# State scan of an audio encoder block: the decayed states' part as one VectorE product with u, and D x summed by TensorE

## Chip, core and metric

The kernel runs on one core of one Trainium2 chip, in float32. The metric is the device time of one execution in microseconds (us). "TensorE", "VectorE", "ScalarE", "GpSimd" and "SyncE" are the core's engines; the profile calls them PE, DVE, ACT, POOL and SP.

## The reference

Three selective-scan layers with a halving of the sequence behind each of the first two, then an attention block and a mixture of experts with 16 experts, each on a normalised input with a residual. The change touches only the scan layers. The input is 32 sequences of 750 steps with 64 channels.

```python
def _ssm_layer(x, A_log, Dp, W_dbc, W_dt, b_dt):
    A = -jnp.exp(A_log)
    dbc = jnp.einsum('ble,ce->blc', x, W_dbc)
    delta, Bm, Cm = jnp.split(dbc, [DT_RANK, DT_RANK + N_STATE], axis=-1)
    delta = jax.nn.softplus(jnp.einsum('blr,er->ble', delta, W_dt) + b_dt)
    dA = jnp.exp(delta[..., None] * A)
    dBx = (delta * x)[..., None] * Bm[:, :, None, :]
    ...
    _, hs = jax.lax.associative_scan(combine, (dA, dBx), axis=1)
    y = jnp.einsum('blen,bln->ble', hs, Cm)
    return y + Dp * x
for i in range(NUM_LAYERS):
    x = _ssm_layer(x, A_log[i], D[i], W_dbc[i], W_dt[i], b_dt[i])
    if i < NUM_LAYERS - 1:
        b, l, d = x.shape
        x = x[:, :l // 2 * 2].reshape(b, l // 2, 2, d).mean(axis=2)
```

## The kernel before

**Tiling.** The 128 partitions hold 64 channels of two sequence groups. A unit is a tile of 128 x 750 (748 in the last layer) steps: 16 units in layer 0, 8 in layer 1, 4 in layer 2, 28 in all. They are taken in eight phases: six of four units (layers 0 and 1) and two of two units (layer 2). Each phase finds out which of the 64 states decay so fast that nothing is left of them a step later. Those are the "decayed" states: their part of y is local, `x * (mixed-down x) * delta`, and needs no scan. The slow ones, two per phase here, are scanned one by one ("slots" 0 and 1, `STATIC = 2`). A branch for more slots (`more_slots`) is in the code and not taken.

**What one unit computes.** With u = delta x (GpSimd, `inputs`):

- decayed part: TensorE multiplies x by a 128 x 128 matrix (`mixed`), VectorE multiplies that by x (`product`), TensorE sums over channels (`summed`), all through the PSUM tile `pairs[3]`. VectorE then multiplies it by delta in place (`by_delta`, L1328), and `output` (L1335) makes y0 = (that + D) x in one instruction. For layers 0 and 1, D and the C weights carry a factor 0.5, since the halving is a mean of two.
- scanned part, for each slot j: TensorE's `weighted_b` into `pairs[1 + j]`, VectorE's `load` (times u, L1343), `recur` (the scan, L1350) and `read` (times C, L1362, into `hC`).
- halving, layers 0 and 1: TensorE's `sums` (L557) adds even and odd columns of both `hC` tiles in one PSUM bank by four products with the identity, two ahead of `weighted_b` of slot 0 of the next unit and two behind it; ScalarE copies the bank out (`sums_out`, L1009); GpSimd adds y0's even and odd columns (L1699) and adds them to that copy (`add`, L1702). In layer 2 there is no halving, and `sums` does nothing.

**Order.** Each engine has a fixed program order, written out in its `period(n)`; semaphores tie the engines together. In a middle period n, VectorE runs load(n,0), product(n+1), recur(n,0), load(n,1), read(n,0), by_delta(n+1), recur(n,1), output(n+1), read(n,1). TensorE runs weighted_b(n,1), row products for later units (L521, L527), summed(n+1), sums(n-1) part 0, weighted_b(n+1,0), sums(n-1) part 1, mixed(n+2); `mixed` waits for `output` of the unit before, since both use `pairs[3]`. At the end of a phase TensorE does sums(n) part 0, weighted_b(n+1,1), sums(n) part 1 at once, so that the last period of a phase has both parts of two units and the first period of the next has none; that first period has the products for the next phase's extremes instead (L506, L564, which wait for VectorE's reduction L1284). GpSimd runs the three steps of delta (L1674, L1677, L1679), then u (L1684), then the halving of the unit before; in a phase's first period the halving stands between delta and u. `wide` (L484, L485) is a product over 750 columns, as 512 and 238.

SyncE brings the C and delta rows in, spread over the partitions (`spread<-rowsd`).

Of the kernel before, what the change touches and what calls it, by code (L numbers as in the profile page):

```python
# [5 lines left out]
ALU = mybir.AluOpType  # L6
# [48 lines left out]
UB = [sum(u for _, _, u in PHASES[:p]) for p in range(NP + 1)]  # L55
# [11 lines left out]


LAST = UB[NP - 1]
Z_OF = UNITS  # L70
ROWS = {-2: [(None, 0), (None, 1)]}
for _n in range(-1, UNITS - 1):
    ROWS[_n] = [(_n + 1, _n + 3 if _n + 3 < LAST else None)]
    if _n == LAST - 3:
        ROWS[_n].append((_n + 2, None))
# [6 lines left out]
def program(nc, a, out):  # L82
    SCALE = float(D) ** 0.25
    with ExitStack() as ctx:
        def sb(name, shape, dt=F32):
            return ctx.enter_context(nc.sbuf_tensor(name, shape, dt))
# [4 lines left out]
        pairs = [ctx.enter_context(nc.psum_tensor(f"pair{i}", [128, 1024], F32)) for i in range(4)]  # L91
        bank = [pairs[i // 2][:, 512 * (i % 2):512 * (i % 2) + 512] for i in range(8)]
# [5 lines left out]
        with nc.sbuf_tensor("spread", [128, 4500], F32) as spread, nc.sbuf_tensor("work", [128, 8400], F32) as work:  # L98
# [7 lines left out]
        delta, u = (big[:, at:at + 750 * RING] for at in (13500, 18750))  # L106

        packed = sb("packed", [128, PACKED])
        ident, blocks, tri, slotno, temp, w0, bdt, dskip, wdt, A = (
            packed[:, at:at + n] for at, n in zip(PACK_AT, PACK))  # L110
# [13 lines left out]
        bproj = sb("bproj", [128, 1])  # L124
        centering = sb("centering", [128, 128])
        averaging = sb("averaging", [128, 128])
        eps = sb("eps", [128, 1])
        zero = sb("zero", [128, 4])
        floor = sb("floor", [128, 16])
# [27 lines left out]
        y0T = [work[:, at:at + 750] for at in (3750, 4500, 5250)]  # L157
# [53 lines left out]
        rw_p, mx_p, s_p, b_p, pl_p = sem("rw_p"), sem("mx_p"), sem("s_p"), sem("b_p"), sem("pl_p")  # L211
        abs_a, relu_a, exp_a, log_a, one_a = sem("abs_a"), sem("relu_a"), sem("exp_a"), sem("log_a"), sem("one_a")
        dk_a, sel_a, rw_a, sm_a = sem("dk_a"), sem("sel_a"), sem("rw_a"), sem("sm_a")
        p_v, t_v, y_v = sem("p_v"), sem("t_v"), sem("y_v")
        bu_v, sc_v, hc_v = sem("bu_v"), sem("sc_v"), sem("hc_v")
        sum_g, cor_g, dl_g, u_g = sem("sum_g"), sem("cor_g"), sem("dl_g"), sem("u_g")
# [76 lines left out]
        def unit(n):  # L293

            p = PH[n]
            l, c, _ = PHASES[p]
            return p, l, WIDTH[l], xcols(l, c + (n - UB[p]) * WIDTH[l], WIDTH[l])

        def of(t, n):
            at = 750 * (n % RING)  # L300
            return t[:, at:at + WIDTH[PHASES[PH[n]][0]]]
# [37 lines left out]
        def after(eng, sem, value):  # L339
            if value > 0:  # L340
                eng.wait_ge(sem, value)

        def halves(t, l):

            if l == 0:
                s = t[:, 0:750].rearrange("p (t k) -> p t k", k=2)
                return s[:, :, 0], s[:, :, 1]
            s = t[:, 0:750].rearrange("p (b t) -> p b t", b=2)[:, :, 0:374].rearrange("p b (t k) -> p b t k", k=2)
            return s[:, :, :, 0], s[:, :, :, 1]

        def parts(t, l):

            return t[:, 0:375] if l == 0 else t[:, 0:374].rearrange("p (b t) -> p b t", b=2)
# [126 lines left out]
        def _(pe):  # L480
# [66 lines left out]

            def sums(n, part):

                _, l, _, _ = unit(n)  # L550
                if l == 2:
                    return
                if part == 0:
                    after(pe, sm_a, TAKEN[n] - 1)
                pe.wait_ge(hc_v, STATIC * n + part + 1)
                for k, t in enumerate(halves(hC[n % 2][part], l)):
                    mm = pe.matmul(parts(bank[1], l), ident, t, start=(part == 0 and k == 0),  # L557
                                   stop=(part == 1 and k == 1))
                if part == 1:
                    mm.then_inc(pl_p, 1)  # L560

# [342 lines left out]
            for l in range(LAYERS):  # L904
                pe.matmul(bank[2][0:64, 128 * l:128 * l + 128].rearrange("p (k c) -> p k c", k=2), wtok[:, l, 1:65],
                          ident[0:64, 0:64].unsqueeze(1).to_broadcast([64, 2, 64]), start=True, stop=True)
                mm = pe.matmul(bank[3][0:64, 128 * l:128 * l + 128].rearrange("p (k c) -> p k c", k=2),
                               wtok[:, l, 65:129], ident[0:64, 0:64].unsqueeze(1).to_broadcast([64, 2, 64]),
                               start=True, stop=True)
            mm.then_inc(setup_p, 1)  # L910
            pe.wait_ge(setup_v, 2)
            for l in range(LAYERS):
                mm = pe.matmul(bank[4][:, l:l + 1], wdtr[0:1, l, :], ident[0:1, 0:1], start=True, stop=True)
# [316 lines left out]
        def _(v):  # L1230
            v.sem_inc(more_v, 1)

            def setup():
                v.memset(w0pm[:, :, :], 0.0)
                v.memset(wZ[:, :, :], 0.0).then_inc(blank_v, 1)
                v.wait_ge(blank_v, 1)
                v.wait_ge(params_in, PARAMS)
                v.tensor_scalar(A, A, 88.0, None, ALU.min)
                v.tensor_scalar(AT[:, :, :], AT[:, :, :], 88.0, None, ALU.min)
                for k in range(2):  # L1240
                    blk = slice(64 * k, 64 * k + 64)
                    v.tensor_copy(w0pm[blk, :, k], w0[blk, :])
                    v.tensor_scalar(w0pm[blk, :, 2 + k], w0[blk, :], -1.0, None, ALU.mult)
                for l in range(LAYERS):
                    for k in range(2):
                        blk = slice(64 * k, 64 * k + 64)
                        ins = v.tensor_scalar(wZ[blk, l, blk], wdt[blk, l, :], w0[blk, l:l + 1], None, ALU.mult)
                ins.then_inc(setup_v, 1)
                for k in range(2):
                    ins = v.tensor_copy(wdtr[:, :, 64 * k:64 * k + 64], wdt[0:1, :, :])  # L1250
                ins.then_inc(setup_v, 1)
                v.tensor_scalar(dskip[:, 0:2], dskip[:, 0:2], 0.5, None, ALU.mult)
                v.tensor_scalar(fscale[:, 0:8], temp, SCALE, None, ALU.mult)
                v.wait_ge(setup_p, 1)
                v.tensor_copy(wBT[:, :, :].rearrange("p l c -> p (l c)"), bank[2][0:64, 0:384])
                v.tensor_scalar(wCT[:, 0:2, :].rearrange("p l c -> p (l c)"), bank[3][0:64, 0:256], 0.5, None, ALU.mult)
                v.tensor_copy(wCT[:, 2, :], bank[3][0:64, 256:384])
                v.wait_ge(setup_p, 2)
                v.tensor_copy(wdtc[:, :], bank[4][:, 0:LAYERS])
                v.wait_ge(setup_a, 2)  # L1260
                v.tensor_scalar(A, A, -1.0, None, ALU.mult)
                v.tensor_scalar(AT[:, :, :], AT[:, :, :], -1.0, None, ALU.mult).then_inc(setup_v, 1)
                v.wait_ge(zeroed, 2)
# [58 lines left out]
                v.tensor_tensor(PT[:, 0:w], pairs[3][:, 0:w], x, ALU.mult).then_inc(p_v, 1)  # L1322

            def by_delta(n):
                _, _, w, _ = unit(n)
                v.wait_ge(s_p, n + 1)
                v.wait_ge(dl_g, n + 1)
                v.tensor_tensor(pairs[3][:, 0:w], pairs[3][:, 0:w], of(delta, n), ALU.mult).then_inc(t_v, 1)  # L1328

            def output(n):  # L1330

                _, l, w, x = unit(n)
                v.wait_ge(t_v, n + 1)
                after(v, xa_g, n - 2)
                v.scalar_tensor_tensor(y0T[n % 3][:, 0:w], pairs[3][:, 0:w], dskip[:, l:l + 1], x, ALU.add, ALU.mult)\  # L1335
                    .then_inc(y_v, 1)

# [557 lines left out]
```

## Time and profile before

| | us |
|---|---|
| median of 3 runs (lowest, highest) | 811.09 (809.99, 812.42) |
| the profiled execution | 812.87 |
| its span in the trace | 810.7 |
| start to the end of unit 0's last instruction on VectorE | 48.67 |
| units 1 to 3 | 32.73 |
| units 4 to 23, five phases of four | 219.35 |
| units 24 to 27 (layer 2) | 55.46 |
| attention and experts | 454.39 |
| TensorE, VectorE, ScalarE, GpSimd busy over the span | 89%, 68%, 52%, 54% |

A stretch's borders are ends of the last `read` (L1362) of a unit on VectorE. In the trace a float32 product shows as two matmul records, so "x4" at L557 is two products. Instructions on one engine overlap at their ends: what one of them takes of the engine is the distance from its start to the next one's start, which is shorter than its duration.

### The profile page before, as it was taken

The page shows a single profiled execution, that of the slowest core. Times are in us where ns is not written, and L with a number is a line of the kernel's source. Part 1 is how long each engine was busy: PE and PEld are TensorE (multiplying, and loading weights), DVE is VectorE, ACT ScalarE, POOL GpSimd, SP SyncE. Part 2 cuts the span into 40 slices and gives each one's busy share as a digit, 9 for nine tenths or more (in the row PEclk, how much of TensorE's full clock was granted, in tenths as well). Part 3 has the DMA queues.
Part 4 walks back from the last instruction along what each step waited for, and adds up shares of the span by engine and source line. Part 5 has one row for each costly group of instructions (what it writes and reads, how often), then busy time and mean ns, then how long its engine had stood idle before and what let it go on. Part 6 is the DMA issues. An engine that isn't in the chain of part 4 may idle for free.

```text
span 810.7 us, 11084 instructions
## 1 busy us (share of the span) xinstructions
PE 721.1 (89%) x3474; PEld 360.3 (44%) x3474; DVE 548.2 (68%) x859; ACT 425.1 (52%) x761; POOL 439.2 (54%) x402
## 2 busy tenths in 40 slices
PE   4789898989899894858999988879999999999997
PEld 2344444545444452326767767733333333333332
DVE  3389899989989897574578888556445445444543
ACT  1778676868786875433445554333433433433432
POOL 1458768686878675845565555243344444434440
PEclk9699999999999997778999999989999999999999
DMA  4446565435344552142000000190954444334400
GB/s 127 137 124 155 125 154 135 120 85 129 92 118 119 129 143 58 39 96 49 1 2 3 4 3 4 29 181 4 197 120 94 102 102 102 86 87 82 108 1 19
DMA packets 30097, 70.20 MB, mean 87 GB/s; under 512 B 4483, under 2 KB 20175, under 8 KB 29647
## 3 DMA queue, kind: packets, MB, share of 16 engines
q1 hardware_dynamic: 29727, 68.77, 35.7%
q8 instruction: 31, 0.51, 0.3%
q10 hardware_dynamic: 304, 0.63, 0.2%
q14 instruction: 35, 0.29, 0.1%
HBM read 66.96 MB, written 2.43 MB: 86 GB/s over the span
## 4 chain that ended last, share of the span: by engine, by line
PE 45%; DVE 8%; ACT 2%; issue 1%; DVEq 0%; ACTq 0%
PE pair L863 22%; PE pair L884 11%; PE pair L766 4%; PE pair L798 3%; PE pair L749 3%; PE pair L785 1%; PE pair L813 1%; DVE big L1489 1%; PE pair L807 1%; ACT big L1153 1%; DVE big L1494 1%; DVE big L1543 0%; DVE big L1554 0%; DVE big L1553 0%; DVE big L1564 0%
## 5 line engine op out<-in xcount | busy, mean ns | idle before, releaser
L1652 DVE TENSOR_TENSOR hidden<-pair,tmp 128x502 f32<-128x502 f32 (+1 forms) x192 | 121.6, 675 | 130.2 <-PE pair L863 105.7
L1778 POOL TENSOR_TENSOR hidden<-xs,big 128x502 f32<-128x502 f32 (+1 forms) x96 | 111.8, 1166 | 169.5 <-PE pair L863 146.9
L1210 ACT ACTIVATE tmp<-pair 128x502 f32<-128x502 f32 (+1 forms) x192 | 102.5, 586 | 157.1 <-PE pair L863 157.1
L1804 POOL TENSOR_TENSOR big<-big 94x512 f32<-94x512 f32 (+3 forms) x120 | 89.1, 775 | 68.0 <-DVE big L1553 58.8
L863 PE MATMUL pair<-xs,w 64*128 64x502 f32 (+1 forms) x384 | 108.1, 640 | 0.5 <-DVE big L1585 0.5
L863 PE MATMUL pair<-hidden,w 64*128 64x502 f32 (+1 forms) x384 | 98.5, 589 | 1.8 <-DVE hidden L1652 1.8
L1350 DVE TENSOR_TENSOR_SCAN pair<-tmp,pair 128x750 f32<-128x750 f32 (+1 forms) x56 | 96.0, 1713 | 0.4
L884 PE MATMUL pair<-hidden,w 128*64 128x502 f32 (+1 forms) x384 | 91.1, 596 | 0.0
L1674 POOL TENSOR_TENSOR big<-big,work 128x750 f32<-128x750 f32 (+1 forms) x28 | 45.6, 1628 | 50.8 <-ACT big L941 50.8
L484 PE MATMUL pair<-big,work 128*128 128x512 f32 x112 | 61.4, 630 | 4.1 <-DVE work L1362 4.1
L863 PEld LDWEIGHTS pair<-xs,w 64*128 64x128 f32 x384 | 29.7, 187 | 67.3 <-issue 36.4
L863 PEld LDWEIGHTS pair<-hidden,w 64*128 64x128 f32 x384 | 37.3, 189 | 48.7 <-issue 46.2
L1343 DVE TENSOR_TENSOR pair<-pair,big 128x750 f32<-128x750 f32 (+1 forms) x56 | 52.1, 931 | 1.5 <-PE pair L485 0.6
L958 ACT ACTIVATE tmp<-big,picked 128x749 f32<-128x749 f32 (+2 forms) x56 | 49.7, 909 | 2.5 <-issue 1.2
L884 PEld LDWEIGHTS pair<-hidden,w 128*64 128x64 f32 x384 | 23.4, 136 | 61.8 <-DVE hidden L1652 34.8
L1702 POOL TENSOR_TENSOR big<-big,work 128x375 f32<-128x375 f32 (+1 forms) x24 | 22.0, 916 | 51.0 <-ACT big L1009 50.6
L1684 POOL TENSOR_TENSOR big<-big 128x750 f32<-128x750 f32 (+1 forms) x28 | 46.7, 1667 | 2.6 <-issue 0.7
L1679 POOL TENSOR_TENSOR big<-big,work 128x750 f32<-128x750 f32 (+1 forms) x28 | 46.2, 1651 | 2.2
L1677 POOL TENSOR_TENSOR work<-work 128x750 f32<-128x750 f32 (+1 forms) x28 | 46.1, 1646 | 1.4 <-ACT work L947 1.4
L766 PEld LDWEIGHTS pair<-big 93*120 93x120 f32 (+1 forms) x384 | 42.2, 184 | 3.1 <-issue 1.5
L766 PE MATMUL pair<-big 93*120 93x65 f32 (+1 forms) x384 | 42.6, 268 | 0.0
L484 PE MATMUL pair<-big,quad 128*128 128x512 f32 x56 | 32.7, 669 | 9.9 <-DVE work L1335 8.8
(185 smaller groups left out, 1268.6 us busy)
## 6 DMA issues: line engine op xcount, KB each, us to landing
big<-dispatched SPq DMA_DIRECT2D x40, 502.0 KB, 6.7
spread<-rowsd SPq DMA_DIRECT2D x48, 375.0 KB, 5.7
spread<-rowsd SPq DMA_DIRECT2D x48, 187.5 KB, 3.4
big<-in_x SPq DMA_DIRECT2D x12, 375.0 KB, 6.1
big<-dispatched SPq DMA_DIRECT2D x8, 498.0 KB, 5.8
spread<-rowsd SPq DMA_DIRECT2D x8, 374.0 KB, 4.9
w<-in_w SPq DMA_DIRECT2D x5, 512.0 KB, 6.8
big<-in_x SPq DMA_DIRECT2D x1, 1500.0 KB, 7.0
```

Of the source, the lines that this page charges most:

```text
L484: pe.matmul(dst[:, 0:512], lhsT, rhs[:, 0:512], start=True, stop=True)
L766: mm = pe.matmul(bank[4 + n % 2][0:FT, at:at + 65], kF[r % 2][0:rows, unit, FT * f:FT * f + FT], qkv[r % 2][0:rows, unit, 143:208], start= ...
L863: pe.matmul(dst[:, 0:hi - lo], weights[blk, HID * e:HID * e + HID], x[blk, :], start=True, stop=True)\
L884: mm = pe.matmul(bank[4][64 * b:64 * b + 64, 0:hi - lo], w3[:, e, :], hidT[(2 * expert + b) % 8][:, 0:hi - lo], start=(e == 0), stop=(e == ...
L958: act.activation(seqs(dA[j], l)[:, :, 1:], seqs(of(delta, n), l)[:, :, 1:], ACT.Exp, scale=picked[p % 2][:, j:j + 1]).then_inc(dk_a, 1)
L1210: act.activation(sT[i % 4][:, 0:w], bank[BANK1[i]][:, 0:w], ACT.Silu).then_inc(silu_a, 1)
L1343: v.tensor_tensor(bu, bu, of(u, n), ALU.mult).then_inc(bu_v, 1)
L1350: v.tensor_tensor_scan(h, dA[j][:, 0:w], h, 0.0, ALU.mult, ALU.add).then_inc(sc_v, 1)
L1652: v.tensor_tensor(hidT[i % 8][:, 0:hi - lo], bank[BANK2[i]][:, 0:hi - lo], sT[i % 4][:, 0:hi - lo], ALU.mult)\
L1684: pool.tensor_tensor(of(u, n), of(delta, n), x, ALU.mult).then_inc(u_g, 1)
L1778: pool.tensor_tensor(xw[e % 4][:, 0:hi - lo], xs[:, lo:hi], wx[:, e, 0:hi - lo], ALU.mult)\
L1804: ins = eng.tensor_tensor(dst[:, :, at:at + H * m].rearrange("p u (h d) -> p u h d", d=m), t[:, :, :, 0:m], t[:, :, :, k:D], ALU.mult)
```

## The change

For layers 0 and 1, `by_delta` is left out, and `output` becomes a plain product of `pairs[3]` with u. It holds the decayed part alone, waits for u (`u_g`) and for `summed` (`s_p`), and no longer for delta. D x is added inside `sums`: two more products per unit (even and odd columns of x) with a diagonal matrix of 0.5 D, one for each layer, which start the accumulation in the PSUM bank. The two matrices are made once in the setup. Layer 2 stays as it was.

```diff
+        diag = sb("diag", [128, 2, 128])
...
-                _, l, _, _ = unit(n)
+                _, l, _, x = unit(n)
                 if l == 2:
                     return
                 if part == 0:
                     after(pe, sm_a, TAKEN[n] - 1)
+                    for k, t in enumerate(halves(x, l)):
+                        pe.matmul(parts(bank[1], l), diag[:, l, :], t, start=(k == 0), stop=False)
                 pe.wait_ge(hc_v, STATIC * n + part + 1)
                 for k, t in enumerate(halves(hC[n % 2][part], l)):
-                    mm = pe.matmul(parts(bank[1], l), ident, t, start=(part == 0 and k == 0),
-                                   stop=(part == 1 and k == 1))
+                    mm = pe.matmul(parts(bank[1], l), ident, t, start=False, stop=(part == 1 and k == 1))
...
-                v.tensor_scalar(dskip[:, 0:2], dskip[:, 0:2], 0.5, None, ALU.mult)
+                for l in range(2):
+                    v.tensor_scalar(diag[:, l, :], ident, dskip[:, l:l + 1], 0.5, ALU.mult, ALU.mult)
...
             def by_delta(n):
-                _, _, w, _ = unit(n)
+
+                _, l, w, _ = unit(n)
+                if l < 2:
+                    return
...
             def output(n):
                 _, l, w, x = unit(n)
-                v.wait_ge(t_v, n + 1)
                 after(v, xa_g, n - 2)
+                if l < 2:
+                    v.wait_ge(s_p, n + 1)
+                    v.wait_ge(u_g, n + 1)
+                    v.tensor_tensor(y0T[n % 3][:, 0:w], pairs[3][:, 0:w], of(u, n), ALU.mult).then_inc(y_v, 1)
+                    return
+                v.wait_ge(t_v, n - LAST_LAYER + 1)
```

The order on TensorE at the end of the second phase, from `mixed` (quad) on: the sums of the last unit around `weighted_b` of slot 1 (pair2). Before:

```order
L484 MATMUL pair<-big,quad 128x512 [waits y_v,dec_v]
L485 MATMUL pair<-big,quad 128x238
L557 MATMUL pair<-work,packed 128x375 [waits hc_v,sm_a]
L557 MATMUL pair<-work,packed 128x375
L484 MATMUL pair<-big,work 128x512 [waits hc_v,sel_a]
L485 MATMUL pair<-big,work 128x238
L557 MATMUL pair<-work,packed 128x375 [waits hc_v]
L557 MATMUL pair<-work,packed 128x375
```

And now, at the same place:

```order
L487 MATMUL pair<-big,quad 128x512 [waits y_v,dec_v]
L488 MATMUL pair<-big,quad 128x238
L559 MATMUL pair<-big,diag 128x375 [waits sm_a]
L559 MATMUL pair<-big,diag 128x375
L562 MATMUL pair<-work,packed 128x375 [waits hc_v]
L562 MATMUL pair<-work,packed 128x375
L487 MATMUL pair<-big,work 128x512 [waits hc_v,sel_a]
L488 MATMUL pair<-big,work 128x238
L562 MATMUL pair<-work,packed 128x375 [waits hc_v]
L562 MATMUL pair<-work,packed 128x375
```

Two products with `diag` stand ahead of the sums, and `weighted_b` of slot 1, for which VectorE's `load` waits, now stands behind four products where it stood behind two.

The order on VectorE in the last period of the first phase, from `load` of slot 1 to the last `read`. Before:

```order
L1343 TENSOR_TENSOR pair<-pair,big 128x750 [waits u_g,b_p]
L1362 TENSOR_TENSOR work<-pair,spread 128x750 [waits pl_p,sc_v,c_d1]
L1328 TENSOR_TENSOR pair<-pair,big 128x750 [waits dl_g,s_p]
L1350 SCALAR_TENSOR_TENSOR pair<-tmp,pair 128x750 [waits bu_v,dk_a]
L1335 SCALAR_TENSOR_TENSOR work<-pair,packed,big 128x750 [waits xa_g,t_v]
L1362 TENSOR_TENSOR work<-pair,spread 128x750 [waits pl_p,sc_v,c_d1]
```

And now:

```order
L1356 TENSOR_TENSOR pair<-pair,big 128x750 [waits u_g,b_p]
L1375 TENSOR_TENSOR work<-pair,spread 128x750 [waits pl_p,sc_v,c_d1]
L1363 SCALAR_TENSOR_TENSOR pair<-tmp,pair 128x750 [waits bu_v,dk_a]
L1345 TENSOR_TENSOR work<-pair,big 128x750 [waits u_g,s_p,xa_g]
L1375 TENSOR_TENSOR work<-pair,spread 128x750 [waits pl_p,sc_v,c_d1]
```

`by_delta` is gone from between the first `read` and the second scan, and its wait for `summed` has moved behind that scan, into `output`, where it is joined by a wait for u.

## Rows read from the trace of the kernel before

**Rows 1.** The page's first part: busy us, share of the span, instructions.

```profile
PE 721.1 (89%) x3474; PEld 360.3 (44%) x3474; DVE 548.2 (68%) x859; ACT 425.1 (52%) x761; POOL 439.2 (54%) x402
```

**Rows 2.** Busy time by stretch; first the five phases of units 4 to 23.

```profile
core 0: us, PE busy (x) PEld busy (x) DVE busy (x) ACT busy (x) POOL busy (x), PEclk, DMA share, GB/s
169.54:212.55 43.01, 39.81 (x162) 20.46 (x161) 39.97 (x50) 33.14 (x53) 32.04 (x25) 1.00 0.46 114
...
sum 219.35, PE 199.64 PEld 101.90 DVE 199.48 ACT 166.04 POOL 163.46; mean PE 39.93 PEld 20.38 DVE 39.90 ACT 33.21 POOL 32.69
```

**Rows 3.** The same for the layer 2 scans and for what comes behind.

```profile
300.75:356.21 55.46, 36.96 (x108) 17.73 (x106) 39.93 (x51) 24.37 (x42) 33.90 (x26) 0.81 0.23 57
356.21:810.60 454.39, 423.18 (x2337) 209.95 (x2336) 258.08 (x483) 184.36 (x372) 200.86 (x216) 0.97 0.30 64
```

**Rows 4.** All waits of TensorE from 81.40 to 300.75: us, times, longest.

```profile
PE pair L564 <- DVE smx L1284: 7.2, 5, 1.6
PE pair L484 <- DVE work L1335: 7.1, 10, 1.6
PE pair L484 <- DVE work L1362: 4.1, 4, 1.3
PE pair L521 <- ACT rows L1002: 0.6, 1, 0.6
PE pair L506 <- POOLq L1728: 0.4, 1, 0.4
PE pair L506 <- POOL big L1702: 0.3, 1, 0.3
```

**Rows 5.** Longest waits of VectorE in the same stretch.

```profile
DVE work L1362 <- DMA spread<-rowsd: 8.2, 6, 2.1
DVE pair L1328 <- PE pair L485: 4.0, 5, 0.8
DVE pair L1328 <- POOL big L1679: 3.4, 4, 1.2
```

**Rows 6.** Timeline of TensorE over a phase's end: start, us, instruction, [idle before].

```profile
209.29 1.50 PE L557 MATMUL pair<-tmp,packed 128*128 128x375 f32 x4
211.85 1.10 PE L484 MATMUL pair<-big,quad 128*128 128x512 f32 x2 [1.07 <-DVE work L1335]
...
213.19 1.49 PE L557 MATMUL pair<-work,packed 128*128 128x375 f32 x4
214.51 1.02 PE L484 MATMUL pair<-big,work 128*128 128x512 f32 x2
...
222.31 0.38 PE L564 MATMUL pair<-packed,smx 128*1 128x128 f32 x2 [1.15 <-DVE smx L1284]
...
223.99 1.02 PE L484 MATMUL pair<-big,quad 128*128 128x512 f32 x2
```

**Rows 7.** Timeline of VectorE there.

```profile
208.25 0.95 DVE L1328 TENSOR_TENSOR pair<-pair,big 128x750 f32<-128x750 f32 x1 [0.61 <-POOL big L1679]
209.11 1.72 DVE L1350 TENSOR_TENSOR_SCAN pair<-tmp,pair 128x750 f32<-128x750 f32 x1
210.73 0.97 DVE L1335 SCALAR_TENSOR_TENSOR work<-pair,packed,big 128x750 f32<-128x750 f32 x1
211.62 0.93 DVE L1362 TENSOR_TENSOR work<-pair,spread 128x750 f32<-128x750 f32 x1
212.47 0.94 DVE L1343 TENSOR_TENSOR pair<-pair,big 128x750 f32<-128x750 f32 x1
...
222.08 0.99 DVE L1335 SCALAR_TENSOR_TENSOR work<-pair,packed,big 128x750 f32<-128x750 f32 x1
```

**Rows 8.** Timeline of GpSimd there: the last halving add, then u.

```profile
218.29 0.99 POOL L1702 TENSOR_TENSOR big<-big,work 128x375 f32<-128x375 f32 x1
219.42 1.79 POOL L1684 TENSOR_TENSOR big<-big 128x750 f32<-128x750 f32 x1
```

**Rows 9.** Groups of VectorE's instructions by line, 81.40 to 300.75.

```profile
L1322 DVE TENSOR_TENSOR work<-pair,big 128x750 f32<-128x750 f32 (+1 forms) x20 | 18.8, 940 | 3.2 <-PE pair L485 3.2
...
L1312 DVE TENSOR_TENSOR quad<-pair,packed 128x128 f32<-128x128 f32 x5 | 1.3, 269 | 0.0
```

**Rows 10.** Timeline of VectorE in the setup and at unit 0's `by_delta`.

```profile
9.55 0.15 DVE L1252 TENSOR_SCALAR packed<-packed 128x2 f32<-128x2 f32 x1
...
11.15 0.16 DVE L1259 COPY wdtc<-pair 128x3 f32<-128x3 f32 x1 [0.40 <-PE pair L913]
...
35.47 0.95 DVE L1328 TENSOR_TENSOR pair<-pair,big 128x750 f32<-128x750 f32 x1 [2.65 <-PE pair L485]
```

More of the change, by code:

```diff
@@ L69 @@
 LAST = UB[NP - 1]
+LAST_LAYER = UB[6]
 Z_OF = UNITS
```

## Prediction

> **What bounds the kernel now.** I read the page's busy shares first [rows 1], but they average over stages, so the next view is busy time by stretch. The change reaches only layers 0 and 1; the stage behind the scans, 454.4 us, is untouched, and so is the work of the layer 2 stretch [rows 3]. In the five phases of units 4 to 23 the two engines that the change moves work between are level: TensorE is busy 39.93 us per phase and VectorE 39.90, of 219.35 / 5 = 43.87, at a granted TensorE clock of 1.00 [rows 2]. ScalarE (33.2) and GpSimd (32.7) have room. So this is not a stage bound by VectorE with TensorE to spare; the reader should see two engines with some 4 us of idle time each in 44, who wait for each other. The third view says how TensorE's idle time is made up. Its waits add up to 7.2 + 7.1 + 4.1 + 0.6 + 0.4 + 0.3 = 19.7 us, or 3.94 per phase, in 22 places [rows 4]. VectorE's longest are for the C rows' transfer (8.2), for `summed` (4.0) and for delta (3.4) [rows 5].
>
> **What the change takes from VectorE.** `by_delta` takes 209.11 - 208.25 = 0.86 us of the engine, start to start. `output` takes 211.62 - 210.73 = 0.89, and as a plain product what its neighbour of the same form takes: `read` at 212.47 - 211.62 = 0.85 [rows 7]; `product` (L1322) has the very operands of the new form, with 940 ns against 970 [rows 7, 9]. Together 0.86 + 0.04 = 0.90 us per unit, 3.6 per phase, 24 x 0.90 = 21.6 us in all.
>
> **What it adds to TensorE.** Two products of 375 columns per unit. The block of two such products at 213.19 is followed by the next at 214.51, so two take 1.32 us and one 0.66 [rows 6]. The diagonal matrix costs no less than the identity: same shape and type. Per phase 4 x 1.32 = 5.28 us, over 24 units 31.7 us. The weight load lies beside the products, as for those that are there.
>
> **The sum per phase.** VectorE: 39.9 - 3.6 = 36.3 us of work in 43.87, so it will wait. TensorE: 39.9 + 5.3 = 45.2, more than the phase takes now. That is the whole argument: TensorE becomes the bound, and only the 3.94 us in which it waits today can take up part of the 5.28.
>
> Which of these waits go? Those for `output` (7.1), for `read` (4.1) and the small ones (1.3) come to 12.5 us, 2.50 per phase. TensorE reaches each with 1.32 us more of work behind it, and VectorE ends `output` 0.90 earlier, so the waits, at most 1.6 long, are covered; I take them as gone. A wait's record also hides the tail of the product ahead of it: the block at 209.29 would have made way at 209.29 + 1.32 = 210.61, the next began at 211.85, so 1.24 was lost where 1.07 is shown [rows 6]. The 17 waits other than the first line's give 17 x 0.17 / 5 = 0.58 per phase more. Together 3.08.
>
> The wait at L564 for the extremes (1.44 per phase) stays. It lies in a phase's first period, in which TensorE has no sums, and its place is told by the rows at 209 to 224. `weighted_b` of slot 1 (214.51) now stands behind two more products; VectorE's load, scan and the reduction for L564 follow from it. Against this 1.32 later start VectorE has 0.86 less to do on the way, and no longer waits there for `summed`. The two about cancel, the period's start is itself later, and I keep 1.44 whole.
>
> So per phase 5.28 - 3.08 = +2.20 us, and for six phases +13.2.
>
> **Edges.** Unit 0's `by_delta` at 35.47 stood behind an idle gap of 2.65 with nothing else to do [rows 10], so there the 0.9 comes off the path. Behind the last phase TensorE has 55.5 - 37.0 = 18.5 us of room in layer 2 [rows 3] and makes up a little of its lateness; I take 0.3. In the setup one small instruction (0.15) gives way to two of 128 x 128 elements; the nearest row of that size is 269 ns [rows 9], so at most +0.4, and VectorE waited 0.40 for TensorE just behind [rows 10]: nothing, and 0.4 if that cover were gone. No transfer and no queue of SyncE is touched; ScalarE's copy of the sums and GpSimd's add come later with the sums' end. Sum: +13.2 - 0.9 - 0.3 = **+12.0 us**. The profiled execution's 812.87 becomes 824.9; it stands 1.8 above the median of the runs, so the median goes from 811.1 to **823 us**.
>
> **The new wait.** `output` waited for `by_delta`, hence for delta; now it waits for u, one GpSimd product (1.79 us) later. Queued behind it on VectorE is `read` of slot 1, and TensorE's `mixed` waits for it. The tight place is a phase's first period, where the halving add stands between delta and u: u is there at 219.42 + 1.79 = 221.21 and `output` starts at 222.08, 0.87 later [rows 7, 8]. That add hangs on the last sums, which end 1.32 later. So u comes at about 222.6 and `output` is some 0.5 late. It would end by 223.6, and `mixed` begins at 223.99 now [rows 6]: covered, with 0.4 to spare. The other periods have u earlier, since u stands ahead of the add there.
>
> **Rivals.**
>
> *Faster: VectorE sets the pace.* If VectorE's order alone fixed the period, 21.6 us would go: 789.5 us. For it: its busy time equals TensorE's [rows 2], and TensorE's two longest kinds of wait are for it [rows 4]. Against it: filling every wait of TensorE gives 3.94 + 22 x 0.17 / 5 = 4.7 us per phase, and 5.28 are added. It decides for this case only if the products take less of TensorE than the distances between starts say.
>
> A rule in the Trainium skill would give this result: "Perfetto Trace Analysis", section "Identifying the Most-Contended Engine", says that matmul busy time is no measure of TensorE's load and that the weight loads' busy share is one of the better ones; the engine with the highest occupancy is to be relieved first. By it TensorE stands at 101.9 / 219.35 = 46% [rows 2] and VectorE at 91%, and the move is a gain. I don't follow it, since the start-to-start distances of [rows 6] show the products themselves filling the engine, with the loads beside them. Chance 0.07.
>
> *TensorE without any wait.* If L564's wait is filled too: +5.28 - 4.7 = +0.6 per phase, +3.5 in all less 1.2 at the edges, +2.3: 813.4 us. It is the floor of what TensorE's work allows, and needs a perfect order; the last period of a phase with its 5.28 us of sums for two units, followed by one with none, speaks against it. Halfway cases fill the room up to my forecast. Chance 0.12 for under 818.
>
> *No wait is filled.* If TensorE and VectorE go strictly in turn, each unit's new products delay everything behind: 31.7 - 1.2 = +30.5, 841.6 us. For it: `mixed` does wait for `output`, and `output` for `summed`, in a ring. Against it: that ring's steps are spread over two periods, with independent work between. Chance 0.06.
>
> *The wait for u decides.* GpSimd's u is later than I have it by over 0.4 us in a phase's first period. Then `mixed` and all behind it move. GpSimd's three steps of delta ahead of it would have to be late as well; now VectorE waits for delta 3.4 us in all [rows 5]. If u came 1.3 later than covered, 6 x 1.3 = 8 us more: 831 us. Chance 0.10.
>
> *The forecast*, 818 to 829, has 0.65. That the change doesn't do what it says is out, as the order shows two products more per unit and one VectorE instruction less.
>
> **How the numbers follow.** Predicted: 823. For 8 in 10, I go down to 815 (most of the second rival; under it lie its very end and the first, about 0.11) and up to 832 (the u case in; above it the strict turns, 0.06). A difference under 0.3%, 2.4 us, is about what a measurement of this kernel can't tell from none. Faster: 0.07. Same, up to 813.5: 0.04, the end of the second rival. Slower: 0.89.
>
> **What would show it.** Right: a phase takes 45.5 to 46.5 us, TensorE's busy time is near 45 of it, its waits for `output` and `read` are almost gone and one before L564 or the row product behind it is left; VectorE's busy time is near 36.3 per phase, and its waits name TensorE, at `product` and at `load`. The stage behind the scans is unchanged within 1 us. Wrong: two products with `diag` take clearly less than 1.32 us of the engine; TensorE still waits some 4 us per phase (strict turns); or VectorE's `output` waits for GpSimd in most periods (the u case). A phase under 43.9 us would mean that VectorE was the bound.

## The result and the profile after

| | us |
|---|---|
| before, median of 4 runs (lowest, highest) | 810.60 (809.99, 812.42) |
| after, median of 4 runs (lowest, highest) | 823.38 (822.74, 826.56) |
| ratio after / before, 95% interval | 1.016 (1.013 to 1.019) |
| the profiled execution after, its span | 823.09, 821.2 |

The change makes the kernel 12.8 us slower; 823 was forecast. The page's first line stands against [rows 1]: TensorE gained 25.3 us of busy time, VectorE lost 20.7.

```profile
PE 746.4 (91%) x3570; PEld 377.6 (46%) x3570; DVE 527.5 (64%) x836; ACT 425.7 (52%) x761; POOL 439.4 (54%) x402
```

Busy time by stretch, with borders at the same instructions as in [rows 2, 3]: units 1 to 3, one of the five phases of units 4 to 23 and their sum, layer 2, and what comes behind.

```profile
core 0: us, PE busy (x) PEld busy (x) DVE busy (x) ACT busy (x) POOL busy (x), PEclk, DMA share, GB/s
48.11:81.05 32.94, 32.94 (x126) 17.67 (x125) 26.95 (x36) 26.09 (x42) 22.75 (x17) 1.00 0.53 139
...
173.07:218.85 45.78, 44.16 (x177) 23.35 (x176) 36.39 (x45) 33.12 (x52) 32.60 (x24) 1.00 0.41 106
...
sum 231.02, PE 223.05 PEld 117.54 DVE 182.66 ACT 166.98 POOL 164.06; mean PE 44.61 PEld 23.51 DVE 36.53 ACT 33.40 POOL 32.81
...
312.07:367.05 54.98, 37.53 (x113) 18.16 (x112) 39.95 (x51) 25.22 (x44) 34.17 (x26) 0.87 0.23 57
367.05:821.20 454.15, 423.18 (x2337) 209.79 (x2336) 258.07 (x482) 184.36 (x372) 200.85 (x216) 0.97 0.30 64
```

Five phases went from 219.35 to 231.02 us, +2.33 each; the scans end at 367.05 instead of 356.21. All of the loss lies there. TensorE is busy 44.61 us of a phase's 46.20, VectorE 36.53.

The waits of TensorE in those five phases, to be held against [rows 4]:

```profile
PE pair L568 <- DVE smx L1289: 6.9, 5, 1.6
PE pair L524 <- ACT rows L1006: 0.6, 1, 0.6
PE pair L509 <- POOLq L1741: 0.3, 1, 0.3
PE pair L509 <- issue: 0.2, 1, 0.2
```

19.7 us have become 8.0. The waits for `output` (7.1) and for `read` (4.1) are gone altogether, the one for the extremes is as it was (7.2, now 6.9). And VectorE's, against [rows 5]:

```profile
DVE work L1327 <- PE pair L488: 13.5, 20, 1.1
DVE pair L1363 <- ACT tmp L962: 7.8, 5, 1.7
DVE pair L1356 <- PE pair L488: 7.6, 10, 1.3
DVE picked L1321 <- PE pair L594: 6.8, 5, 1.4
DVE work L1375 <- DMA spread<-rowsd: 6.6, 5, 1.8
DVE work L1345 <- POOL big L1697: 4.1, 4, 1.2
```

VectorE now waits for TensorE at `product` (L1327) in all 20 periods and at `load` (L1356) in ten. At the same phase's end as in [rows 6], TensorE's timeline shows why: not one gap from the sums at 217.52 to the row products, and two products with `diag` that take 221.44 - 220.11 = 1.33 us.

```profile
217.52 1.50 PE L562 MATMUL pair<-tmp,packed 128*128 128x375 f32 x4
218.85 1.02 PE L487 MATMUL pair<-big,quad 128*128 128x512 f32 x2
219.71 0.57 PE L488 MATMUL pair<-big,quad 128*128 128x238 f32 x2
220.11 1.48 PE L559 MATMUL pair<-big,diag 128*128 128x375 f32 x4
221.44 1.48 PE L562 MATMUL pair<-work,packed 128*128 128x375 f32 x4
222.76 1.02 PE L487 MATMUL pair<-big,work 128*128 128x512 f32 x2
...
227.82 1.47 PE L509 MATMUL pair<-big,w0pm 128*32 128x375 f32 x16 [0.29 <-POOLq L1741]
230.44 0.38 PE L568 MATMUL pair<-packed,smx 128*1 128x128 f32 x2 [1.15 <-DVE smx L1289]
```

So the 2.33 can be written as an account of TensorE alone: busy +4.68 per phase, waits -2.34.

### The profile page after: what moved, and what is told of

The parts are those of the page before. It is cut to its first block, busy times and chain, and to the rows that moved or that the text cites. A ratio compares the mean times of both kernels' runs of the same rounds, so it can differ in the third digit from the quotient of the medians.

```text
span 821.2 us, 11209 instructions
## 1 busy us (share of the span) xinstructions
PE 746.4 (91%) x3570; PEld 377.6 (46%) x3570; DVE 527.5 (64%) x836; ACT 425.7 (52%) x761; POOL 439.4 (54%) x402
## 4 chain that ended last, share of the span: by engine, by line
PE 45%; DVE 8%; ACT 2%; issue 1%; DVEq 0%; ACTq 0%
PE pair L867 21%; PE pair L888 11%; PE pair L770 4%; PE pair L802 3%; PE pair L753 3%; PE pair L789 1%; PE pair L817 1%; DVE big L1502 1%; PE pair L811 1%; ACT big L1157 1%; DVE big L1507 0%; DVE big L1556 0%; DVE big L1567 0%; DVE big L1566 0%; DVE big L1577 0%
## 5 line engine op out<-in xcount | busy, mean ns | idle before, releaser
L1356 DVE TENSOR_TENSOR pair<-pair,big 128x750 f32<-128x750 f32 (+1 forms) x56 | 52.1, 931 | 9.8 <-PE pair L488 9.8
L802 PE MATMUL pair<-big 120*64 120x188 f32 x384 | 38.4, 354 | 1.9 <-issue 1.2
```

What stands on the lines that cost most here:

```text
L802: mm = pe.matmul(dst[64 * b:64 * b + 64, TOK * k:TOK * k + TOK], kvm[n % 2][:, k, FTN * b + f, :], qT[n % 2][:, f, TOK * b:TOK * b + TOK], ...
L1356: v.tensor_tensor(bu, bu, of(u, n), ALU.mult).then_inc(bu_v, 1)
```

## The experiments

Single executions of one kernel differ by some microseconds, and much of that lies in the untouched stage behind the scans (449.6 to 461.0 us over the profiled executions of this section). Layer 2, whose own work is unchanged, took 53.6 to 57.7 us in them, and the first phase depends on TensorE's clock (see item 4 of the next section). The kernel before had medians of 812.41, 810.98 and 811.13 beside the first four, the next four and the last two kernels. So beside the median of the runs I give the end of the scans in the profiled execution, on VectorE: 356.21 before, 367.05 after. It still holds layer 2 and the first phase, so that a difference of 2 us in it says little; the five phases alone are the cleaner measure, 219.35 before and 231.02 after.

### Each half of the change alone

The VectorE half: the changed kernel without the products, so that D x is left out.

```diff
-                    for k, t in enumerate(halves(x, l)):
-                        pe.matmul(parts(bank[1], l), diag[:, l, :], t, start=(k == 0), stop=False)
...
-                    mm = pe.matmul(parts(bank[1], l), ident, t, start=False, stop=(part == 1 and k == 1))
+                    mm = pe.matmul(parts(bank[1], l), ident, t, start=(part == 0 and k == 0), stop=(part == 1 and k == 1))
```

> The changed kernel without the two products with the diagonal matrix, so D x is left out of layers 0 and 1. VectorE has the change's 0.90 us less per unit, TensorE the work of before. Theory A (before, TensorE and VectorE are level and wait for each other; the other one takes over as soon as one gets lighter): TensorE's 39.9 us of records per phase plus some 0.7 of hidden tails is 40.6, and the wait for the extremes of 1.4 stays, so a phase goes from 43.9 to about 42 to 42.5 and the whole comes to 802 to 805, a quarter to a half of VectorE's 21.6. Rival B (VectorE alone sets the pace before, and every saved microsecond counts): 811 - 21.6 = 789.

Median 802.28, ratio to before 0.987 (0.983 to 0.992), end of the scans 346.27. The sum of its five phases:

```profile
sum 215.11, PE 199.05 PEld 101.93 DVE 182.97 ACT 166.95 POOL 164.08; mean PE 39.81 PEld 20.39 DVE 36.59 ACT 33.39 POOL 32.82
```

With VectorE at 36.59 and TensorE at its old 39.81, a phase takes 43.02 (42 to 42.5 expected): of 3.3 us taken off VectorE 0.85 arrive. Rival B, VectorE as the one bound of the kernel before, falls: 789 was its time.

The TensorE half: the kernel before, with products with a zero matrix.

```diff
                 if part == 0:
                     after(pe, sm_a, TAKEN[n] - 1)
+                    for k, t in enumerate(halves(x, l)):
+                        pe.matmul(parts(bank[1], l), diag[:, l, :], t, start=(k == 0), stop=False)
...
+                for l in range(2):
+                    v.tensor_scalar(diag[:, l, :], ident, 0.0, None, ALU.mult)
```

> The kernel before with the two diagonal products per unit added, their matrix being zero, and VectorE's instructions as before (by_delta is there, D x is added by output). Complete result. Theory A (TensorE alone paces the changed kernel): as the changed kernel or up to 4 us above it, 823 to 828, since VectorE's 39.9 us of a phase fit beside TensorE's 44.6 to 45.2. Rival C (the two halves of the change add up, each worth its own time): the changed kernel plus what the VectorE half is worth alone, so plus 6 to 20, 829 to 843. If the products delayed all behind them (strict turns) it would be 811 + 31.7 = 843.

Median 826.83, ratio 1.018 (1.014 to 1.023); the profiled execution was a long one (span 835.1), with 461.0 us in the untouched stage and the scans' end at 374.09. The medians are 3.5 us apart from the changed kernel's. The five phases took 233.75, 2.7 us more than in the changed kernel:

```profile
sum 233.75, PE 222.98 PEld 116.59 DVE 199.91 ACT 166.81 POOL 164.11; mean PE 44.60 PEld 23.32 DVE 39.98 ACT 33.36 POOL 32.82
```

In them TensorE waits for `output` again, which it never does in the changed kernel:

```profile
PE pair L486 <- DVE work L1340: 2.3, 6, 0.5
```

So beside the products VectorE's saving is worth some 0.5 us per phase, where it is worth 0.85 without them. The 0.5 rests on one execution, 10.2 us above its kernel's median, of which the untouched stage explains 6.8. The halves don't add up: alone the VectorE half gave 10 us against the kernel before, and under rival C it would have given the same here, where the medians differ by 3.5. Strict turns would have given 843.

### From none to three products

One product per unit (even columns of x; D x of the odd columns is left out), and three (the third with a zero matrix):

```diff
-                    for k, t in enumerate(halves(x, l)):
+                    for k, t in enumerate(halves(x, l)[0:1]):
```

```diff
...
+                    pe.matmul(parts(bank[1], l), blank[:, :], halves(x, l)[0], start=False, stop=False)
```

> The changed kernel with the product for the even columns of x alone; D x of the odd columns is left out. TensorE has 0.66 us less per unit, 2.64 per phase, 15.8 in all. Theory A (TensorE paces): most of it comes off, 809 to 812. Rival D (a ring through other engines holds the changed kernel, and TensorE is only busy within it): under half comes off, 816 or more.

> The changed kernel with a third product per unit beside the two diagonal ones, its matrix zero: 0.66 us more of TensorE per unit, 2.64 per phase, 15.8 in all. Complete result. In the steps from none over one to two products the end of the scans moved by 7.3 and 13.5 us, 46% and 85% of 15.8. Theory A (waits fill up first, then TensorE's work is the time): the third step is dearer than the second, 14 to 15.8 us, so 837 to 840 us, and TensorE's waits other than for the extremes stay near zero. Rival D (some ring takes a fixed share of each step): 46% to 85% again, 831 to 837.

| products per unit | end of the scans | step | five phases | step | median |
|---|---|---|---|---|---|
| 0 | 346.27 | | 215.11 | | 802.28 |
| 1 | 353.57 | 7.3 | 220.18 | 5.1 | 812.91 |
| 2 (the change) | 367.05 | 13.5 | 231.02 | 10.8 | 823.38 |
| 3 | 382.90 | 15.9 | 243.29 | 12.3 | 839.43 |

Each step adds 24 x 0.66 = 15.8 us of TensorE's time, 13.2 of it in the five phases. In the five phases the share that shows rises from 38% over 82% to 93%, at the end of the scans from 46% over 85% to all of it: the first product goes mostly into waits, the third costs nearly its whole time. That is what theory A says and what a ring with a fixed share doesn't. The medians bear out only the last step: 10.6, 10.5 and 16.0 us, so two thirds, two thirds and all. The profiled execution with one product was one of the fastest of its ten, 2.9 us below their median; that the second product costs more than the first rests on one execution of each kernel. One product came out at 812.91, a little above the 809 to 812 expected; its ratio to before is 1.003 (0.999 to 1.006), the point where the VectorE saving and the products balance. With three products TensorE's waits are:

```profile
PE pair L575 <- DVE smx L1297: 7.3, 5, 1.6
PE pair L525 <- ACT rows L1013: 0.6, 1, 0.6
```

### Are the weight loads the load?

The changed kernel with five of the six products of a unit's sums cut in two: 11 instead of 6, over the same columns.

```diff
...
-                    mm = pe.matmul(parts(bank[1], l), ident, t, start=False, stop=(part == 1 and k == 1))
+                    for c in range(2):
+                        mm = pe.matmul(cut(parts(bank[1], l), l, c), ident, cut(t, l, c), start=False,
+                                       stop=(part == 1 and k == 1 and c == 1))
```

> The changed kernel, in which the second diagonal product and the four products with the identity of a unit are each cut into two halves of the columns: 11 products per unit where there were 6, the same 2250 columns, and the weight loads of the sums nearly doubled (20 more of two records of 0.19 us per phase, 7.6 us on 23.5). Complete result. Theory A (columns fill TensorE, the loads lie beside them): a product more costs only the few hundredths by which start-to-start exceeds the columns, 20 x 0.03 = 0.6 us per phase, so 2 to 6 us above the changed kernel, 825 to 829. Rival L (the weight loads' busy time is the load of TensorE): 20 x 0.38 = 7.6 us per phase, 46 in all, toward 860.

Median 823.39, the changed kernel's time, and a little under the 825 to 829 expected by theory A; end of the scans 368.64, 1.6 later. In the stretch of the five phases (81.05 to 312.07, as cut for the changed kernel) the weight loads' busy time rose from 117.54 to 146.48 us, and a block of four half-width products still gives way after 215.73 - 214.40 = 1.33 us:

```profile
81.05:312.07 231.02, 222.46 (x1076) 146.48 (x1075) 181.84 (x220) 166.30 (x262) 163.93 (x120) 1.00 0.47 116
```

```profile
214.40 1.49 PE L572 MATMUL pair<-tmp,packed 128*128 128x188 f32 x8
215.73 1.02 PE L487 MATMUL pair<-big,work 128*128 128x512 f32 x2
```

Rival L falls: 29 us more of weight loads cost nothing that can be measured. Columns are what fills TensorE here.

### What holds the remaining wait

TensorE's 6.9 us at L568 stayed, as forecast, but through what? The prediction traced it to `weighted_b` and `load`. First test: of a phase's last unit, the products with `diag` stand behind that `weighted_b`.

```diff
-                if part == 0:
+                late = last_of(n) is not None
...
+                if part == int(late):
                     for k, t in enumerate(halves(x, l)):
-                        pe.matmul(parts(bank[1], l), diag[:, l, :], t, start=(k == 0), stop=False)
+                        pe.matmul(parts(bank[1], l), diag[:, l, :], t, start=(k == 0 and not late), stop=False)
...
-                    mm = pe.matmul(parts(bank[1], l), ident, t, start=False, stop=(part == 1 and k == 1))
+                    mm = pe.matmul(parts(bank[1], l), ident, t, start=(late and part == 0 and k == 0), stop=(part == 1 and k == 1))
```

> The changed kernel, in which the two diagonal products of a phase's last unit stand behind weighted_b of slot 1 and not ahead of it, so that VectorE's load of slot 1 in the next phase's first period can start 1.32 us earlier. The work is the same. Theory E (as the prediction had it: the wait at the extremes, 6.9 us in five phases of the changed kernel, comes down from that load): the wait shrinks to nothing, a phase gets up to 1.3 us shorter, 816 to 818. Rival F (it comes down from the last sums' end, by ScalarE's copy and the decay of slot 1 behind it, for which the scan waits 7.8 us in five phases): the sums' end stays where it is, so 822 to 824, and the wait for the decay grows by what the load's wait loses.

Median 826.16 (822.99 to 832.46), ratio 1.017 (1.010 to 1.024): no gain. The five phases took 230.70 us, 0.3 less than in the changed kernel, where theory E promised up to 6.5; the scans ended at 372.08, 5.0 later, of which 3.0 lie in the first phase (item 4 of the next section). The waits say it more sharply; TensorE's first line, then VectorE's:

```profile
PE pair L570 <- DVE smx L1291: 6.9, 5, 1.6
```

```profile
DVE pair L1365 <- ACT tmp L964: 14.4, 5, 3.0
...
DVE pair L1358 <- PE pair L488: 1.0, 5, 0.2
```

`load`'s wait fell from 7.6 to 1.0, the scan's wait for the decay rose from 7.8 to 14.4, and L570 still waits 6.9. Theory E, the prediction's, falls. Second test: the decay ahead of ScalarE's copy of the last sums.

```diff
-                if j == 1 and n == UB[p] and p:
-                    act.wait_ge(more_v, MV[p])
...
-                if n >= 0:
+                if n >= 0 and (n == 0 or last_of(n - 1) is None):
                     decay(n, 1)
...
                 if last_of(n) is not None:
+                    if nxt:
+                        decay(n + 1, 1)
                     sums_out(n)
                     more_slots(last_of(n))
```

> The changed kernel; on ScalarE the decay of slot 1 for a phase's first unit stands ahead of the copy of the last sums, not behind it and behind the branch for more slots. (The branch, not taken here, would need it again behind itself; that part is left out.) Work and all other orders are the same. Theory F (the wait of TensorE for the extremes comes from the last sums' end through this decay): the scan no longer waits 7.8 us in five phases for it, TensorE's 6.9 us for the extremes are gone, with some hidden tail 1.4 us per phase, so 7 to 8 us below the changed kernel, 815 to 817. Rival G (another wait stands right behind, for u or for the next product, and gives the same time): less than 2 us below the changed kernel.

Median 822.35 (817.49 to 823.98), 1.0 below the changed kernel's where 7 to 8 were expected; end of the scans 365.98, 1.1 earlier, five phases 229.51, 1.5 less: theory F falls too. The scan no longer waits for the decay, but the reduction behind it does, for TensorE's own row products (L509); TensorE's and VectorE's lines:

```profile
PE pair L568 <- DVE smx L1289: 5.4, 5, 1.2
```

```profile
DVE smx L1289 <- PE pair L509: 6.4, 5, 1.7
```

```profile
224.24 1.71 DVE L1363 TENSOR_TENSOR_SCAN pair<-tmp,pair 128x750 f32<-128x750 f32 x1
227.66 0.94 DVE L1289 TENSOR_REDUCE smx<-pair 128x1 f32<-128x750 f32 x1 [1.72 <-PE pair L509]
```

So two things hold it: TensorE makes the row products, VectorE reduces them (0.94 us), and TensorE's next instruction in order needs the result. In the changed kernel the scan, late by the decay, and the row products end together: the scan at 227.50 + 1.73 = 229.23, the row products at 227.82 + 1.47 = 229.29, the reduction starts at 229.35. With the scan earlier the row products still hold the reduction, as decay_early shows; that the scan would hold it if the row products came earlier follows from the two ends and was not run. The there-and-back of some 1.1 us (5.4 in five phases) stays.

```profile
227.50 1.73 DVE L1363 TENSOR_TENSOR_SCAN pair<-tmp,pair 128x750 f32<-128x750 f32 x1 [1.50 <-ACT tmp L962]
229.35 0.94 DVE L1289 TENSOR_REDUCE smx<-pair 128x1 f32<-128x750 f32 x1
```

(These two are of the changed kernel.) It can only be filled. So the third test puts work into it: the `diag` products of a phase's first unit, from one period later to right ahead of L568.

```diff
-                    for k, t in enumerate(halves(x, l)):
+                    for k, t in enumerate(halves(x, l) if chain(n)[1] != 0 else ()):
...
                     extreme_rows(p, pairs[1]).then_inc(dec_p, 1)
                     pe.wait_ge(rw_a, EVENT_AT[n + 1])
+                    d_sums(n)
```

> The changed kernel; the two diagonal products of a phase's first unit stand in that unit's own period, right ahead of the product for the extremes (where TensorE waits 6.9 us in five phases), and not one period later with the other sums. Work is the same, 1.32 us of it moved into a wait of 1.15 plus a hidden tail of 0.17. Theory A (TensorE's own work plus this one wait is the whole of a phase): 1.3 us per phase, 7 to 8 us below the changed kernel, 815 to 817. Rival D (a ring through other engines holds it): no gain, 822 to 825.

Median 819.29 (818.47 to 820.57), ratio to before 1.010 (1.006 to 1.015), end of the scans 365.00. The 6.9 us are gone, yet the five phases shrank by 1.5 us, not 6.5:

```profile
PE pair L487 <- DVE work L1382: 3.2, 4, 1.2
```

```profile
227.10 1.58 PE L570 MATMUL pair<-big,diag 128*128 128x374 f32 x4
228.62 0.38 PE L574 MATMUL pair<-packed,smx 128*1 128x128 f32 x2
```

Two things took most of it back. In the period from which the products were taken, TensorE now reaches `weighted_b` before `read` is done, which itself waits for the transfer of the C rows: 3.2 us of a wait that was 4.1 before the change and that the products had hidden. And the block at 227.10 takes 228.62 - 227.10 = 1.52 us and not 1.32, 1.0 in five phases. What is left of the missing 5.0, 0.8 us, fits the hidden tails of the four waits, 4 x 0.17 = 0.7. Waits fell by 3.7 (8.0 to 4.3), busy time rose by 2.2 (223.05 to 225.25), which is the 1.5. Of the median's 4.1 us only 2.05 lie in the scans of the profiled execution, and the intervals of the two ratios (1.006 to 1.015 here, 1.013 to 1.019 for the changed kernel) overlap.

### A version that beats both

If only what lies in a wait is free, the change should be made where the wait is. Only the first unit of each phase has the new form, with its products right ahead of the product for the extremes, as in d_in_wait; the other three are computed as before. The second kernel has the early decay of decay_early besides.

```diff
+def NEWF(n):
+    return n < LAST_LAYER and (n % 4 == 0)
...
-                if l < 2:
+                if NEWF(n):
...
```

> Complete result. Only the first unit of each phase has the change's form (y0 times u, two diagonal products), with its products placed in TensorE's wait for the extremes as in the run d_in_wait; the other three units of a phase are computed as before. VectorE has 0.9 us less per phase, TensorE 1.32 more, which lie in a wait of 1.44 of the kernel before. Theory A (what lies in a wait is free, and the lighter VectorE gives a third of its saving, as vector_half showed): 6 x 0.3 to 6 x 0.9, so 2 to 5 us below the kernel before, 806 to 809. Rival C (the products cost their time wherever they stand): 6 x 1.32 less 2, so 6 us above it, 817.

> As one_in_four, and on ScalarE the decay of slot 1 for a phase's first unit ahead of the copy of the last sums (with the same part left out as in decay_early). In the kernel before that decay ends at 219.23 and by_delta at 219.51, so the scan is held by by_delta, which waits for summed. Theory: no gain from the decay, within 1 us of one_in_four. Rival: the decay holds it there too: 4 to 8 us below one_in_four.

| | median of 12 runs | ratio to before | end of the scans |
|---|---|---|---|
| one_in_four | 807.27 | 0.997 (0.994 to 1.000) | 348.30 |
| one_in_four_early | 806.38 | 0.994 (0.992 to 0.996) | 350.70 |

The sums over the five phases of one_in_four, against 219.35 before:

```profile
sum 215.17, PE 206.65 PEld 105.06 DVE 196.31 ACT 166.52 POOL 164.06; mean PE 41.33 PEld 21.01 DVE 39.26 ACT 33.30 POOL 32.81
```

7 us more of TensorE's time went into waits, and a phase is 0.8 us shorter (0.4 in one_in_four_early). Both kernels gain some 4 us, 0.3% and 0.6%, the first just clear of no change, the second clearly. They can't be told apart: the second has the lower median by 0.9 us, and its scans ended 2.4 us later. That is as expected, and in neither does the scan wait for the decay. one_in_four keeps the branch for more slow states; one_in_four_early, like decay_early, leaves out what that branch needs.

One rival was not run: the same one unit in four with its products in their ordinary place. In the table above one product per unit, which is more work for TensorE than this, went in part into waits without being placed. So it isn't shown how much of the gain is due to the place and how much to the smaller amount.

## Why the prediction was right

Its mechanism held, and its sum was 824.9 for the profiled execution, which took 823.09: +10.2 us where +12.0 was forecast. That the median came out at 823.38 against 823 is in part luck, since the profiled execution before stood 2.3 us above its median of four runs and the one after 0.3 below.

1. *TensorE becomes the bound.* Shown by the waits of both engines and by the third product, which cost nearly all of its time. Two products take 1.33 us of the engine (1.32 forecast). VectorE's busy time per phase is 36.53 (36.3 forecast), a phase 46.20 (45.5 to 46.5).
2. *Waits for `output` and `read` go, 3.08 per phase with their hidden tails.* They did: the records of waits fell by 2.34 per phase, and busy time rose by 4.68, 0.60 less than the products' 5.28, which are the tails (0.58 forecast). Net +2.33 against +2.20. The 17 waits did not all go, the small ones among them stayed at 1.1 us in all.
3. *The extremes' wait stays.* Right in size (6.9 of 7.2), wrong in what holds it. The prediction's chain by `weighted_b` and `load` isn't the one: in d_behind the wait for it was gone and the 6.9 stayed. decay_early shows the round trip from the row products by VectorE's reduction under it.
4. *Six phases at +2.20.* The term that was mis-sized. The first phase's units 1 to 3 took 32.73 us before and 32.94 now, +0.2 and not +2.2. Most of the difference is TensorE's granted clock, which in this stretch was 0.95 before and 1.00 now:

```profile
48.67:81.40 32.73, 31.88 (x115) 16.30 (x115) 29.51 (x39) 25.88 (x43) 22.33 (x17) 0.95 0.53 138
```

Around the stretch's start the kernel before ran some instructions at 1.2 GHz instead of 2.4, behind a wait of 2.89 us:

```profile
47.07 0.38 PE L564 MATMUL pair<-packed,smx 128*1 128x128 f32 x2 [2.89 <-DVE smx L1284]
...
48.34 1.00 PE L485 MATMUL pair<-big,work 128*128 128x238 f32 x2
49.14 1.92 PE L484 MATMUL pair<-big,quad 128*128 128x512 f32 x2
50.84 1.00 PE L485 MATMUL pair<-big,quad 128*128 128x238 f32 x2
51.77 0.38 PE L568 MATMUL pair<-sext,wdtr 1*128 1x2 f32 x2
```

From 48.34 to 51.77 are 3.43 us. In the changed kernel the same instructions take 49.59 - 47.83 = 1.76:

```profile
47.83 0.57 PE L488 MATMUL pair<-big,work 128*128 128x238 f32 x2
...
49.59 0.38 PE L572 MATMUL pair<-sext,wdtr 1*128 1x2 f32 x2
```

The lower level cost 1.67 us, some 1.5 of them behind the border at 48.67. TensorE was busy 31.88 us of that stretch's 32.73, so they show nearly in full: about 1.5 of the 2.0 us are the clock's. Two more kernels ran at the lower level there, tensor_half (first row below) and d_behind (second row):

```profile
49.00:84.12 35.12, 35.12 (x129) 18.89 (x128) 29.64 (x38) 25.87 (x44) 22.12 (x17) 0.97 0.51 130
49.09:85.00 35.91, 35.91 (x128) 19.17 (x127) 26.96 (x36) 25.41 (x42) 22.06 (x17) 0.93 0.49 126
```

In this stretch d_behind has the changed kernel's work, and took 3.0 us more. tensor_half, whose clock fell like that of the kernel before, took 2.4 us more than that kernel, close to the 2.2 forecast for a phase. TensorE's longest wait ahead of the slow instructions was 2.89, 3.04 and 2.12 us in these three, and at most 1.8 at this place in the nine others, which had 1.00. No run isolates what brings the clock down, nor how often each kernel meets it. vector_half and one_in_four, with 30.18 and 30.35 us at 1.00, are 2.4 to 2.6 below the kernel before, where a later phase gained 0.8: most of the rest is again the clock's.

5. *Edges.* Unit 0's end came 0.56 earlier (0.9 forecast), layer 2 took 0.48 less (0.3), the stage behind 0.24 less (0), and what lies outside the span, 2.27 before and 1.89 now, 0.38 less (0). Against the forecast these are +0.34, -0.18, -0.24 and -0.38; with the first phase's -2.0 and the five phases' +0.65 they make up the 1.8 us between sum and measurement. Layer 2 took 54.98 here and 56.3 to 56.4 in d_behind, decay_early and d_in_wait, with the same work, so its agreement is chance.
6. *The wait for u is covered.* VectorE's `output` waits 4.1 us for GpSimd in the five phases, in four places, and TensorE never waits for `output`. In the tight period VectorE does the reduction (at 229.35) first: u ends at 229.39, `output` starts at 230.21. So the half microsecond of lateness that was forecast there didn't come.
7. *The rule on the weight loads.* The Trainium skill's "Perfetto Trace Analysis", section "Identifying the Most-Contended Engine", names the weight loads' busy share as one of two measures of TensorE's room; by it TensorE, at 46%, had room. That doesn't hold for this kernel's float32 products, and the measurement decides: split_products raised that share from 51% to 63% at no cost, and three_products cost nearly its whole time at a share of 51% (124.81 of 243.29).

The expectations of one_product, d_in_wait and decay_early were too hopeful: the medians lie 0.9, 2.3 and 5.4 us above the upper ends of their ranges. For the last two a second wait stood right behind the one that was removed; for one_product no run shows why.

## What to carry to other kernels

Where two engines are level and wait for each other, moving work from one to the other is a loss as soon as the work is dearer there than the second engine's waits are long: count the receiver's idle time per period first, since it is all that the move can use. A wait's length is what is saved only if nothing ends right behind it; look up the second and third latest before paying for the first. Then make the move only for the instances whose new work falls into a wait; here that, with a quarter of the work moved, turned a loss of 12.8 us into a gain of some 4.

## What the hardware showed unexpectedly

A product cut into two of half the columns costs the same (1.33 us for four of 188 and 187 columns, 1.32 for two of 375), with twice the weight loads. In d_in_wait the block of two products that stands between products of other output widths took 1.52 us instead of 1.32 (why was not tested). TensorE's clock level at the same place differed between kernels with the same work there: one stretch of units 1 to 3 took 32.94 us at a granted clock of 1.00 and 35.91 at 0.93.
